# Moving two expert products on TensorE and one finishing addition on VectorE in a gated mixture-of-experts kernel

## The reference

```python
x = x + conv_gate(_ln_c(x))      # _ln_c: layer norm over the 64 channels of a pixel
#   conv_gate(z): pooled = [max over channels, mean over channels]; 3x3 conv to one plane; z * sigmoid(plane)
t = _to_tokens(x)                # a token per pixel, 64 channels
t = t + ffn(_ln_t(t))            # ffn(z): softmax router over 8 experts, the two best, their weights made to sum to 1,
#   sum over the two of weight * (z @ expert_w[e] + expert_b[e])
x = _from_tokens(t, x)
```

## Time and profile before

| | |
|---|---|
| median of 3 runs | 1424.98 us |
| the profiled execution | 1424.37 us, its span 1422.6 us |
| TensorE busy | 1310.0 us, 92% of the span |
| VectorE busy | 1240.8 us, 87% |
| ScalarE busy | 1054.4 us, 74% |
| GpSimd busy | 1069.4 us, 75% |
| DMA share of 16 engines | 60.6% |
| granted TensorE clock, mean | 0.97 of full speed |

### The profile page before, as it was taken

How to read it: one execution, slowest core, us unless ns; L and a number is a source line. 1 busy time by engine, 2 the same in 40 slices (tenths; PEclk the granted TensorE clock), 3 DMA queues, 4 the chain that set the end, 5 groups by cost and what they waited for, 6 DMA issues and landing times.

```text
span 1422.6 us, 33089 instructions
## 1 busy us (share of the span) xinstructions
PE 1310.0 (92%) x11750; PEld 616.6 (43%) x11750; DVE 1240.8 (87%) x1527; ACT 1054.4 (74%) x3949; POOL 1069.4 (75%) x643
## 2 busy tenths in 40 slices
PE   8954999999999999999999999999999988899998
PEld 8853444444444444444444444444444322333332
DVE  5786799979999899988999899988999889987776
ACT  6567898888988898888988899888897334444442
POOL 5334787887788787887887887887888886887765
PEclk9955999999999999999999999999999999999999
DMA  6442466666667667676666666576665555566663
GB/s 220 121 124 81 133 205 195 195 195 203 203 187 219 190 209 211 174 224 195 195 182 216 190 209 204 175 231 198 200 197 156 156 156 156 156 178 185 175 189 117
DMA packets 85845, 259.97 MB, mean 183 GB/s; under 512 B 13744, under 2 KB 13744, under 8 KB 85680
## 3 DMA queue, kind: packets, MB, share of 16 engines
q1 hardware_dynamic: 85680, 257.85, 60.6%
HBM read 206.42 MB, written 51.38 MB: 181 GB/s over the span
## 4 chain that ended last, share of the span: by engine, by line
PE 53%; DVE 24%; issue 12%; POOL 2%; ACT 1%; DVEq 0%; POOLq 0%; ACTq 0%
PE moe L561 31%; DVE gx L703 15%; PE gb L507 8%; PE tm L486 8%; PE tm L500 2%; DVE ge L725 2%; PE moe L555 2%; DVE stats L680 2%; PE tm L546 1%; DVE ot L716 1%; DVE oh L738 1%; PE tm L585 1%; DVE u L788 1%; POOL dl L1235 1%; DVE early_s L680 0%
## 5 line engine op out<-in xcount | busy, mean ns | idle before, releaser
L561 PE MATMUL moe<-gx,wc 128*64 128x448 f32 x3584 | 813.4, 554 | 0.0
L703 DVE TENSOR_TENSOR gx<-gb,xd 128x896 f32<-128x896 f32 x672 | 707.3, 1085 | 85.6 <-PE gb L507 84.8
L1175 POOL TENSOR_TENSOR gx<-gs,xd 128x896 f32<-128x896 f32 x224 | 494.1, 2206 | 250.8 <-ACT gs L990 195.8
L990 ACT ACTIVATE gs<-gb 128x896 f32<-128x896 f32 x224 | 205.3, 916 | 193.9 <-PE gb L507 188.5
L952 ACT ACTIVATE sq<-xct 112x64 f32<-112x64 f32 x1400 | 338.4, 246 | 7.8 <-DVE early_s L690 2.1
L561 PEld LDWEIGHTS moe<-gx,wc 128*64 128x64 f32 x3584 | 217.9, 136 | 195.0 <-issue 162.0
L952 ACT ACTIVATION_READ_ACCUMULATOR sq<-xct 112x1 f32 x1400 | 265.4, 190 | 0.0
L507 PE MATMUL gb<-s,cg 32*128 32x448 f16 x1792 | 186.6, 360 | 64.5 <-DVE gx L703 63.3
L1192 POOL TENSOR_TENSOR tt<-xc,a1s 128x896 f32<-128x896 f32 x112 | 235.5, 2103 | 11.4 <-issue 9.7
L507 PEld LDWEIGHTS gb<-s,cg 32*128 32x128 f16 x1792 | 51.0, 91 | 402.5 <-DVE gx L703 336.4
L486 PE MATMUL tm<-rhs,xa 64*112 64x74 f32 x2800 | 184.6, 272 | 11.8 <-ACT logit_mean L937 8.4
(11 more groups left out here) (93 smaller groups left out, 1091.7 us busy)
## 6 DMA issues: line engine op xcount, KB each, us to landing
xd<-in_x_dram SPq DMA_DIRECT2D x448, 224.0 KB, 4.1
xa<-in_x_dram SPq DMA_DIRECT2D x112, 448.0 KB, 4.5
xc<-in_x_dram SPq DMA_DIRECT2D x112, 448.0 KB, 4.7
out_dram<-ot SPq DMA_DIRECT2D x112, 448.0 KB, 3.6
gx<-in_const_g_dram SPq DMA_DIRECT2D x1, 384.0 KB, 4.7
cf<-in_const_f_dram SPq DMA_DIRECT2D x1, 333.5 KB, 2.8
cf<-in_L_ffn_expert_b_dram SPq DMA_DIRECT2D x12, 1.0 KB
gx<-in_L_ffn_expert_w_dram SPq DMA_DIRECT2D x1, 128.0 KB, 4.5
```

Of the source, the lines that this page charges most:

```text
L561: last = pe.matmul(moe[b * CH:(b + 1) * CH, c, 0:HALF], wc[:, k * CH:(k + 1) * CH], gx[:, u, b, :], start=False, stop=(k == KT - 1), skip_ ...
L703: dve.tensor_tensor(gx[:, i, :, :], gb[:, 2 * slot:2 * slot + 2, 0:HALF], xd[:, v % 2, :, c * HALF:(c + 1) * HALF], ALU.mult).then_inc(sca ...
L990: act.activation(gs[:, j, :, :], gb[:, 2:4, 0:HALF], ACT.Copy).then_inc(gate_out, 1)
L1175: pool.tensor_tensor(gx[:, ND + j, :, :], gs[:, j, :, :], xd[:, v % 2, :, j * HALF:(j + 1) * HALF], ALU.mult).then_inc(scaled_p, 1)
```

## The change

Three blocks of code are moved; nothing is added or removed.

- TensorE, `body`: product 5 of the step before (`experts_of_dve(r, v - 1, 5)`) moves from behind the first spreading batch to ahead of it.
- TensorE, `body`: product 2 (`experts_of_dve(r, v, 2)`) moves from behind the third batch (and, in step 2 of a round with part B, the convolution) to ahead of it.
- VectorE, `body`: the second finishing addition of the step before (`finish(r, v - 1, 1)`) moves from behind unit 1 to ahead of it.

```diff
+                    if on(r, v - 1):
+                        experts_of_dve(r, v - 1, 5)
                     if cur:
                         spread_for_dve(r, v, 1)
                         spread_for_pool(r, v, 1)
-                    if on(r, v - 1):
-                        experts_of_dve(r, v - 1, 5)
                     if ahead:
                         turn(r, step, v + 1)
...
                     if cur:
+                        experts_of_dve(r, v, 2)
                         spread_for_dve(r, v, 4)
                     if ahead:
                         spread_for_pool(r, v + 1, 0)
                     if Bp and step == 2:
                         convolve(r, A)
-                    if cur:
-                        experts_of_dve(r, v, 2)
                     if ahead:
                         spread_a1(r, step, v + 1, A, Bp)
...
                     if Bp:
                         gate(r, step, False)
+                    if on(r, v - 1):
+                        finish(r, v - 1, 1)
                     if cur:
                         scale_unit(r, v, 1)
-                    if on(r, v - 1):
-                        finish(r, v - 1, 1)
```

## The result

The changed kernel takes 1488.36 us, the median of four runs (1487.44 to 1489.52); the kernel before, on the same chip, 1424.81. The ratio is 1.0441, 95% interval 1.0423 to 1.0459: slower. The forecast was 1476, range 1450 to 1508. The profiled execution took 1489.52 us.

What follows compares the result with a forecast made beforehand. Three engines are nearly full, so hand-over order decides, with ScalarE's copies without slack before `centre_rows`. Full rounds +69, rounds 9 and 10 -18, round 8 0: +51 us on 1424.98 gives 1476, range 1450 to 1508.

Steps and rivals of the forecast that it cites:

- The main term: Full rounds: ScalarE's copies hold back `centre_rows`, so a plain step costs +1.07 us on 83 steps, +89 us.
- round 8: Router pieces on VectorE, no part A: gains and losses taken as equal, 0, with ends of -10 and +20 us.
- The plain step: A step whose router pieces delay nobody: first half +0.75, second half +0.32, together +1.07 us.
- The relief from waits for VectorE: Full rounds: TensorE's waits for VectorE shrink by 3.3 us per round, 20 us in six rounds, ends 0 and 35.
- the term for the full rounds: Full rounds: +89 us for plain steps less 20 us of shrunken waits for VectorE, +69 us.
- The addition's gap: VectorE idles 0.46 us between units 1 and 2 without the finishing addition; costed at nothing in a plain step.
- Rounds 9 and 10: No part A: product moves gain 0.74 and 0.5 us per half, -1.25 per step, -18 us over some 15 steps.
- Rival 2: ScalarE's copies aren't a limit, VectorE's gap decides: full rounds +22 us, late rounds -18, 1429 us; chance 0.04.
- Rival 1: GpSimd locks out VectorE's router operations once more per full round: 32 us more, 1508 us; chance 0.12.
- rival 3: Three products in a row cover VectorE's lateness at no cost: 35 us and 18 us gained, 1372 us; chance 0.07.
- rival 4: Nothing measurable: gain in late rounds and loss in early ones cancel, 1425 us; chance 0.03.

## Why the prediction was right, and where it was off

The sum was +51 and the time grew by 63.6 (1488.36 less 1424.81). The main term holds by its mechanism; 8 us of the rest are relief that was taken too high, and 8 are round 8, whose term of 0 had its sources only in part.

**The plain step.** Predicted +1.07, measured 1.07 (11.99 against 10.92). The single moves gave 0.76 and 0.32 against 0.75 and 0.32. The step of the working that carries the case, that `centre_rows` can come no sooner than 2.88 behind the first batch because three copies stand in one queue behind it, was shown three ways: the distance is 2.88 after too; it shrinks to 2.32 when parts is taken out of it; and the plain step is the same 11.99 with the finishing addition at its old place.

**The relief from waits for VectorE.** Predicted 3.3 us per round, measured 1.9 (14 x 1.07 less 13.1); over six rounds that is the 8 us by which the term for the full rounds (+69, measured +77.3) fell short. The large waits shrank as told (steps of 12.18 to 12.94, i.e. +0.76 instead of +1.07). Two things worked against it. The convolution step cost 1.43, for the sigmoid that product 2 had covered (0.6 us per round in the list of waits). And the finishing addition had a price in two router steps per round (12.54 and 12.53, against 11.99 and 12.00 without it). There the router piece itself came to lie behind a GpSimd operation:

```profile
756.15 2.10 POOL L1191 TENSOR_TENSOR tt<-xc,a1s 128x896 f32<-128x896 f32 x1
...
757.36 1.37 DVE L729 TENSOR_TENSOR key<-ge,prio 112x896 bf16<-112x896 bf16 x1
```

The piece took 0.66 before; now VectorE gets to the addition and unit 1 so late that they show. With the addition at its old place the piece is as long (1.35) and the step is 11.99 all the same, so it takes both. I had costed the addition at nothing on the cover of a plain step; that cover is short in these two. It is thinner than I had it in the plain step too: I had unit 1 end at 1.75 and the second batch follow at 1.85, measured are 2.27 and 2.32, because VectorE is in a router piece of its own until 746.97. `centre_rows` could have started at 748.94 (748.64 + 0.30), 0.26 ahead of where s let it.

**The addition's gap.** Told to be 0.46 and hidden: it is 0.46 and hidden in the plain step. Rival 2 priced it at 22 us; undoing the move gave 1.0 per full round, 6 in all.

**Rounds 9 and 10.** -18 predicted, -18.5 measured in round 9, and -19.0 when done alone, with 8.91 per step.

**Round 8.** Predicted 0 with ends of -10 and +20, measured +7.6. Two things that are uneven from kernel to kernel make it up, and the prediction had only the first, and that only in its range. Operations of VectorE's router were held up by GpSimd: 7.19 and 2.88 us before, 8.66 and 6.91 after, 5.5 more; each kernel of this study drew another set. And behind long waits TensorE's products ran at the lower clock: two stretches before (3.25 and 2.90 us for two products that take 1.72), four after (4.17, 3.85, 4.63 and 4.11 for three that take 2.48), a loss of 2.7 and of 6.8. Two of the four stand in the first two steps of the round, where no operation of VectorE is held up for 5 us: TensorE waits 2.69 and 2.24 for unit 4 there, where it waited 1.24 and 1.02 with product 2 still behind the third batch. The rest of the new order's effect, its gain in steps without a heavy piece (8.95 instead of 10.24) first of all, is against these two.

The two waits of GpSimd don't end all this. With them round 8 takes 155.8 in the old order and 161.6 in the new one, 5.8 more. In the old order no stretch is then at the lower clock; in the new one there are four (4.17, 3.77, 3.73 and 4.17), a loss of 5.9. That accounts for the size of the difference; that gains and longer waits beside it cancel is read off the traces, and no run takes them apart.

**The rivals.** Rival 1 came true in small, in round 8 only, not in the full rounds, where the longest such piece took 1.87 us. Rivals 2, 3 and 4 are excluded by the two single product moves. What rival 3 had for it was right in one place: in the late rounds TensorE no longer stops for unit 3. That is half of their gain, 0.71 per step with product 2 alone; the other half is product 5's, 0.62 alone.

**Not settled.** That the lower clock and unit 4 hold the steps named above is read from traces; no run removes the lower clock alone, or the stretched `ge` in steps 6, 10 and 12.

## What to carry to other kernels

When a producer's batch feeds another engine's queue, ask what stands in that queue behind the batch and who waits for its last entry: filling the producer's stalls with work ahead of the batch delays all of it. If a hand-over ends within 0.1 or 0.2 us of its use, it has no slack, whether or not the profile books a wait. The same edit can be right in one stage and wrong in another; here it cost 1.07 per plain step where `centre_rows` waits for ScalarE's copies and gave 1.3 in rounds 9 and 10, which have no `centre_rows`, so it belongs in the second stage only. And look at the granted clock behind each long wait: TensorE can pay for it again in the work that follows.

## What the runs showed of the hardware

VectorE's operations with both inputs in SBUF were held up by GpSimd for longer than one operation: one that started at 1243.22 by the profile let four operations of GpSimd go by that started after it, and took 8.66 us. It ended 0.94 us after GpSimd paused. One semaphore wait in GpSimd's queue, which makes such a pause, cut the same piece from 7.22 to 3.08 us in the kernel with the moves in rounds 9 and 10 only. By the Trainium skill (SBUF — State Buffer, section "Who interferes with whom") the one that issues first has the shared ports for the whole instruction and the other blocks until it has finished. The exclusion agrees with these rows. The rule for one instruction doesn't give their length, though, nor the 7.19 us that the prediction took to agree with it: GpSimd's queued operations went ahead of the blocked one as long as they followed one another without a pause.

TensorE's granted clock fell to the lower level behind waits of 7.61, 6.74, 2.69 and 2.24 us in round 8 of the changed kernel, and three products then took 3.85 to 4.63 us instead of 2.48. The length of the wait alone doesn't tell: behind one of 1.37 us it fell too (4.17 us, in the kernel with s ahead of parts), and behind one of 2.28 us in the changed kernel with GpSimd's two waits it stayed up (2.48 us).
